# Graph network kernel: general visits of the counts at the head, degrees and bias ahead of a last scatter done by halves, GpSimd left with the gathers

## The chip, the cores and the metric

One Trainium2 chip, one core. The metric is the device time of one execution in microseconds; the number shown is the median of several runs. The profile is that of one execution, and its times are microseconds from the start of its span.

## What is computed

There are 1024 nodes of 128 features and 32768 edges, sorted by their destination. Two layers follow each other, each with a residual. The first is a message-passing layer, the second a graph convolution:

```python
h = jnp.maximum(_layernorm(x), 0.0)
messages = mlp3(concat[h[src], h[dst], edge_attr])
summed = segment_sum(messages, src) + segment_sum(messages, dst)
attention = concat[paired[:, 0] - paired[:, 1], paired[:, 1] - paired[:, 0]]
x = x + mlp3(concat[h, summed, attention])
h = jnp.maximum(_layernorm(x), 0.0)
deg = segment_sum(ones, col)                  # edges and one loop per node
norm = rsqrt(deg)[row] * rsqrt(deg)[col]
x = x + gelu(segment_sum(norm * (h @ W)[row], col) + b)
```

## The kernel before

**Head.** The first layer of the message network is taken apart: `h` times the source and the destination part of `mW1` gives two tables of 1024 x 256, which go to memory. GpSimd gathers their rows for the edges, 128 at a time, by indirect DMAs (L451, L459). Beside this TensorE makes the node's own part of the update (`update_of_node`, L558), ScalarE adds its bias (L895), and VectorE works out from the sorted destinations in which tiles of edges each window lies (L1186 to L1211, turned into a row by `turn_starts`, L511). It then makes the middles and half gaps of the edges' ends (`middles`, L1213).

**Loop over groups.** A group is 512 edges, four tiles of 128; there are 64. The loop is unrolled, and each engine has its own order of a group's steps, written out by hand (`group`, L689 for TensorE, L857 for ScalarE, L1042 for VectorE). In group g TensorE does the second layer of g (L612), the first layer of g + 1 (edge part L592, transposes of the gathered rows L598), the messages of g (L622), and scatters the messages of g - 1 (L640) into two banks that hold the sums for 512 nodes each. For the scatter of a tile an incidence matrix of 128 edges x 1024 nodes is made: ScalarE takes the distance of each node from the middle of the edge's ends (L827), VectorE compares it with the half gap (L1039). For the last tile of a group ScalarE makes the incidence itself in two further passes (L833, L842). For tiles 0 and 2 VectorE's operands are laid out in three rows of 342 (`IN_ROWS`). VectorE also adds the two gathered rows of each edge (`add_pairs`, L1080), makes the low parts of numbers that are multiplied in two parts (L1013, L1019, L1025), and TensorE's first transpose of a group waits for the first half of `add_pairs`.

**Counts.** The graph convolution needs the matrix of edge counts, 1024 x 1024 (`ct_sb`), and the degrees. The destinations are cut into 32 windows of 32 nodes, each window into ten tiles of edges. For each tile VectorE makes two one-hot matrices (`one_hot`, L1088 and L1089), and TensorE multiplies them in among the transposes (`count_tile`, L658). A window takes two groups, five tiles in each; VectorE makes the one-hots a group ahead. When a window is done, ScalarE copies its counts out of PSUM (`window_out`, L887), and VectorE sums them by rows and by columns (`window_sums`, L1108, L1110). Where a window has more than ten tiles, the rest is added by general visits in a loop whose length is read at run time (`more_windows`, L663 and L1113); it always makes at least one visit. It stands after the last window, between the second layer of group 63 and the scatter behind it.

**End.** After it TensorE sums the column counts (`count_ends`, L676), VectorE makes the degrees and the bias times the number of messages (`degrees`, L1174), and TensorE adds that to the sums after the last scatter (`add_bias_of_sums`, L684). ScalarE copies one half of the sums (L904), VectorE the other (L1270), and the update (L726, L732, L740), the second layer norm, the product with the counts (L777) and the output follow. GpSimd, after its last gather, adds the last update bias to `x` (L479) and the identity to the diagonal of the counts (L484, L486).

**What sets the order.** Engines run their instructions in order and wait on semaphores. The queue of SP holds the loads, two loads of edges per group, and the stores; GpSimd's holds the gathers. A gather waits only for its ring buffer of three groups (`GB`).

## Time and profile before

| | us |
|---|---|
| median of 3 runs | 765.26 |
| the runs | 765.11, 765.26, 767.28 |
| the profiled execution, its own time | 768.67 |
| its span | 766.8 |
| busy: TensorE | 741.0 (97%) |
| busy: VectorE | 688.5 (90%) |
| busy: ScalarE | 650.0 (85%) |
| busy: GpSimd | 540.6 (71%) |

Share is of the span. In the rows PE is TensorE, PEld its weight loads, DVE is VectorE, ACT ScalarE, POOL GpSimd. A line number after L is the line of the kernel before. An entry in square brackets at the end of a timeline's row is the idle time of the engine just before that instruction, and what released it. Rows of the chain give net time along the chain, so that an instruction which overlaps the one before it counts only with what it adds. "Granted clock" is the share of TensorE's full clock, 1.00 for 2.4 GHz and 0.50 for 1.2 GHz.

### The profile page before, as it was taken

What the parts mean: (1) busy time and instruction counts of PE and PEld (TensorE: products, weight loads), DVE (VectorE), ACT (ScalarE), POOL (GpSimd) and SP (SyncE); (2) the same over time, 40 slices, a digit from 0 to 9 for tenths busy, and PEclk for the clock granted to TensorE, in tenths of its full rate; (3) what the DMA queues carried; (4) which work ended last, traced back from release to release, by engine and by line L of the source; (5) the groups of instructions that cost most, each with busy time, mean ns of one, the idle gap of its engine ahead of it and who ended that gap; (6) DMA issues with size and microseconds to landing.
All of it is one profiled execution on the core that took longest, in us unless ns stands there. A gap on an engine that the chain in (4) does not pass through costs nothing.

```text
span 766.8 us, 13408 instructions
## 1 busy us (share of the span) xinstructions
PE 741.0 (97%) x4171; PEld 624.5 (81%) x4171; DVE 688.5 (90%) x1444; ACT 650.0 (85%) x839; POOL 540.6 (71%) x533
## 2 busy tenths in 40 slices
PE   7589999999999999999999999999999999999996
PEld 6468888888888888888888888888888888888755
DVE  7869899999999999899998999989999999999765
ACT  3358899999999999999999999999999999998843
POOL 3677777777777777777777777777777777777100
PEclk9789999999999999999999999999999999999999
DMA  8434334444344443344434444344433444442000
GB/s 230 152 115 127 118 112 126 136 125 129 113 124 130 121 133 114 116 134 128 126 109 125 131 131 125 111 123 131 131 122 107 130 135 128 123 118 84 1 0 28
DMA packets 42566, 90.15 MB, mean 118 GB/s; under 512 B 11136, under 2 KB 17920, under 8 KB 42496
## 3 DMA queue, kind: packets, MB, share of 16 engines
q0 software_dynamic: 24576, 67.14, 28.8%
q1 hardware_dynamic: 17920, 22.16, 9.9%
q8 instruction: 33, 0.54, 0.3%
q14 instruction: 37, 0.30, 0.1%
HBM read 86.64 MB, written 2.62 MB: 116 GB/s over the span
## 4 chain that ended last, share of the span: by engine, by line
PE 85%; POOL 7%; issue 2%; DVE 2%; DMA 1%; ACT 1%; DVEq 0%; SPq 0%; POOLq 0%
PE bank L640 29%; PE bank L612 21%; PE bank L622 14%; PE bank L592 7%; PE bank L598 7%; PE bank L658 4%; POOL rows_sb L451 3%; POOL rows_sb L459 3%; PE bank L732 1%; PE bank L777 1%; DMA table_a<-rows_sb 1%; DMA rows_sb<-table_b,ends_i 1%; PE bank L740 1%; PE bank L726 0%; DVE rows_sb L960 0%
## 5 line engine op out<-in xcount | busy, mean ns | idle before, releaser
L459 POOL DMA_INDIRECT rows_sb<-table_b,ends_i x256 | 266.8, 1042 | 78.0 <-issue 78.0
L451 POOL DMA_INDIRECT rows_sb<-table_a,ends_i x256 | 261.4, 1021 | 83.7 <-issue 77.7
L827 ACT ACTIVATE dist<-iota_h,neg_mid 128x1026 f16<-128x1026 f16 (+1 forms) x256 | 294.1, 1150 | 0.0
L1039 DVE TENSOR_SCALAR ring<-dist,half_gap,times 128x1026 fp32r<-128x1026 f16 (+1 forms) x192 | 224.7, 1171 | 0.3 <-ACT dist L827 0.3
L640 PE MATMUL bank<-ring,m_hi 128*128 128x512 f32 x512 | 172.8, 419 | 0.1
L640 PE MATMUL bank<-ring,m_lo 128*128 128x512 f32 x512 | 161.6, 397 | 0.0
L612 PE MATMUL bank<-ring,w_hi 128*128 128x512 f32 x512 | 151.3, 397 | 1.4 <-DVE ring L1019 1.4
L814 ACT ACTIVATE h_sb<-bank,b_sb 128x512 f32<-128x512 f32 x128 | 87.5, 684 | 59.1 <-PE bank L612 59.1
L1089 DVE TENSOR_SCALAR oh_key<-iota_h,key_f,minus_base 128x258 bf16<-128x258 f16 x321 | 128.9, 401 | 0.0
L622 PE MATMUL bank<-w_sb,h_sb 128*128 128x128 f32 x1024 | 125.8, 276 | 0.0
L598 PE MATMUL bank<-ident,rows_sb 128*128 128x128 f32 x512 | 114.3, 277 | 8.0 <-DVE rows_sb L1080 8.0
L622 PEld LDWEIGHTS bank<-w_sb,h_sb 128*128 128x128 f32 x1024 | 120.7, 193 | 0.2
L612 PEld LDWEIGHTS bank<-ring,w_hi 128*128 128x128 f32 x512 | 96.9, 190 | 24.6 <-DVE ring L1019 2.0
L640 PEld LDWEIGHTS bank<-ring,m_lo 128*128 128x128 f32 x512 | 97.5, 190 | 23.3
L1019 DVE SCALAR_TENSOR_TENSOR ring<-bank,ring 128x512 fp32r<-128x512 f32 x128 | 88.3, 690 | 26.6 <-ACT ring L808 25.0
L1080 DVE TENSOR_TENSOR rows_sb<-rows_sb 128x512 f32<-128x512 f32 x128 | 84.2, 685 | 25.0 <-DMA rows_sb<-table_b,ends_i 24.9
L640 PEld LDWEIGHTS bank<-ring,m_hi 128*128 128x128 f32 x512 | 87.7, 191 | 11.7 <-issue 0.2
L1088 DVE TENSOR_SCALAR oh_low<-iota_h,low_f 128x128 bf16<-128x128 f16 x321 | 86.5, 270 | 2.4 <-issue 2.3
L808 ACT ACTIVATE ring<-bank 128x512 fp32r<-128x512 f32 x128 | 76.1, 594 | 14.3 <-PE bank L598 14.3
L598 PEld LDWEIGHTS bank<-ident,rows_sb 128*128 128x128 f32 x512 | 70.6, 143 | 20.2 <-DVE rows_sb L1080 10.2
L612 PE MATMUL bank<-ring,w_lo 128*128 128x512 f32 x256 | 80.8, 397 | 0.0
L842 ACT ACTIVATE ring<-dist,times,neg_times 128x1024 fp32r<-128x1024 f16 x64 | 79.5, 1243 | 0.1
(186 smaller groups left out, 783.6 us busy)
## 6 DMA issues: line engine op xcount, KB each, us to landing
e_raw<-edge_attr_t SPq DMA_DIRECT2D x128, 128.0 KB
rows_sb<-table_a,ends_i POOLq DMA_INDIRECT x256, 2.8
rows_sb<-table_b,ends_i POOLq DMA_INDIRECT x256, 2.9
table_a<-rows_sb SPq DMA_DIRECT2D x4, 256.0 KB, 3.5
table_b<-rows_sb SPq DMA_DIRECT2D x4, 256.0 KB, 3.0
x_sb<-x SPq DMA_DIRECT2D x2, 256.0 KB, 3.3
out<-oh_key SPq DMA_DIRECT2D x4, 128.0 KB, 1.8
u_sb<-uW SPq DMA_DIRECT2D x1, 384.0 KB, 5.0
```

Source lines behind the costliest of these rows:

```text
L451: nc.gpsimd.indirect_dma_start(got[:, b, t, 0, :], None, table_a, bass.IndirectOffsetOnAxis(ap=ends_i[:, 0, tile:tile + 1], axis=0),).then ...
L459: nc.gpsimd.indirect_dma_start(got[:, b, t, 1, :], None, table_b, bass.IndirectOffsetOnAxis(ap=ends_i[:, 1, tile:tile + 1], axis=0),).then ...
L598: mm = nc.tensor.matmul(z1t_bank[k][:, t * P:(t + 1) * P], got[:, g % GB, t, 0, part], ident[:, :], start=False, stop=True, is_transpose=T ...
L612: mm = nc.tensor.matmul(z2_bank[m][:, :], w[:, k, m * P:(m + 1) * P], a[:, b, k, :], start=(n == 0), stop=(n == len(parts) - 1))
L622: mm = nc.tensor.matmul(msg_bank[:, t * D:(t + 1) * D], h2_sb[:, k, t * P:(t + 1) * P], w3_sb[:, k, :], start=(t == 0 and k == 0), stop=(k ...
L640: mm = nc.tensor.matmul(acc_bank[n][:, :], part[:, b, t, :], inc[:, t, n * HB:(n + 1) * HB], start=(is_first(g) and t == 0 and part is m_h ...
L814: nc.scalar.activation(h2_sb[:, m, :], z2_bank[m][:, :], ACT.Relu, bias=b2_sb[:, m:m + 1]).then_inc(h2_ready, 1)
L827: nc.scalar.activation(to, of, ACT.Abs, bias=neg_mid[:, bass.ds(g * GT + t, 1)]).then_inc(dist_ready, 1)
L1019: nc.vector.scalar_tensor_tensor(h1_lo[:, b, k, :], z1t_bank[k][:, :], 0.0, h1_hi[:, b, k, :].bitcast(F32), ALU.max, ALU.subtract).then_in ...
L1039: nc.vector.tensor_scalar(to, of, half_gap[:, tile], times[:, tile], ALU.is_equal, ALU.mult).then_inc(inc_ready, 1)
L1088: nc.vector.tensor_scalar(oh_low[:, slot, j, :], iota_h[:, 0:P], low_f[:, bass.ds(tile, 1)], None, ALU.is_equal)
L1089: return nc.vector.tensor_scalar(oh_key[:, slot, j, :, 0:KN], iota_h[:, 0:KR * KN].rearrange("p (r n) -> p r n", r=KR), key_f[:, bass.ds(t ...
```

## The change

**Order of the counts.** Half-windows take the place of windows in the loop. Half-window h is counted in group h (before: in group h - 1); in groups 16, 33 and 48 two half-windows are counted, so that the last is counted in group 60 (before: 62). VectorE makes a half-window's one-hots a group ahead, interleaved as before; the second one of a doubled group is made in one piece at the end of VectorE's group.

```diff
-LAST_W = 2 * (NW - 1)
...
-def made_in(i):
...
-    return 0 <= i and i + 1 < NW
...
-def summed_in(b, i):
...
-    return b == 0 and 0 <= i < NW
+TWICE = (16, 33, 48)
...
+def counted_in(g):
...
+    first = g + sum(g > x for x in TWICE)
+    found = (first, first + 1) if g in TWICE else (first,)
+    return [h for h in found if 0 <= h < HALVES]
...
+def made_in(g):
...
+    return counted_in(g + 1)
...
+def summed_in(g):
...
+    found = [h // 2 for h in counted_in(g) if h % 2]
+    return found[0] if found else None
...
+LAST_SUM = HALVES - 1 - len(TWICE)
...
+def all_on_vector(g):
...
+    return g >= GROUPS - 2
...
+def in_rows(g, t):
...
+    return t in IN_ROWS and not all_on_vector(g)
```

**GpSimd.** What stood behind the gathers is taken out.

```diff
-    pool.wait_ge(ld_w, 16 * 12)
-    nc.gpsimd.tensor_tensor(xb_sb[:, :, :], x_sb[:, :, :],
-                            ub3_all[:, :].unsqueeze(1).broadcast_to([P, NC, D]), ALU.add).then_inc(xb_ready, 1)
...
-    pool.wait_ge(into_ready, 1)
-    diagonal = ct_all[:, 0:(NC - 1) * (N + P)].rearrange("p (s n) -> p s n", n=N + P)[:, :, 0:P]
-    nc.gpsimd.tensor_tensor(diagonal, diagonal, ident[:, :].unsqueeze(1).broadcast_to([P, NC - 1, P]), ALU.add)
-    diagonal = ct_all[:, (NC - 1) * (N + P):NC * N]
-    nc.gpsimd.tensor_tensor(diagonal, diagonal, ident[:, :], ALU.add).then_inc(self_added, 1)
```

**TensorE.** The row of window starts is turned inside the update of nodes, the general visits come ahead of the loop, the count of ends goes into group 61, and the last scatter is done for the first 512 nodes and then for the others, behind the bias.

```diff
+        if k == KH * NH - 2:
+            turn_starts()
...
-                count_tile(counting[0], counting[1] * (VT // 2) + t - COUNTS_AT[k][0] + k * len(COUNTS_AT[0]))
+                count_tile(counting[0], t + k * len(COUNTS_AT[0]))
...
+        if k == KH - 1:
+            for h in counting[1:]:
+                for j in range(HALF):
+                    count_tile(h, j)
...
     def wait_incidence(g, t):
-        if t < DT:
+        if all_on_vector(g):
+            pe.wait_ge(inc_ready, DT * (GROUPS - 2) + GT * (g - GROUPS + 2) + (t + 1))
+        elif t < DT:
...
-    def counts_of(g):
...
-        w = (g + 1) // 2
-        return (w, (g + 1) % 2) if 0 <= w < NW else None
...
-    def count_tile(w, j):
...
-        if j % (VT // 2) == 0:
-            pe.wait_ge(w_hot, 2 * w + j // (VT // 2) + 1)
+    def count_tile(h, j):
...
+        w, j = h // 2, h % 2 * HALF + j
+        if j % HALF == 0:
+            pe.wait_ge(w_hot, h + 1)
...
     def more_windows():
-        pe.wait_ge(w_out, NW)
...
-            mm = nc.tensor.matmul(acc_bank[c // 4][:, (c % 4) * P:(c % 4 + 1) * P], cb3[:, c, :], ident[:, :],
-                                  start=False, stop=(c % 4 == 3), is_transpose=True, skip_group_check=True)
-            if c % 4 == 3:
-                mm.then_inc(sums_ready, 1)
+            nc.tensor.matmul(acc_bank[c // 4][:, (c % 4) * P:(c % 4 + 1) * P], cb3[:, c, :], ident[:, :],
+                             start=False, stop=False, is_transpose=True, skip_group_check=True)
...
+    def last_scatter(g, b):
...
+        pe.wait_ge(m_lo_ready, g + 1)
+        for n in range(NH):
+            for t in range(GT):
+                if n == 0:
+                    wait_incidence(g, t)
+                for part in (m_hi, m_lo):
+                    mm = nc.tensor.matmul(acc_bank[n][:, :], part[:, b, t, :], inc[:, t, n * HB:(n + 1) * HB],
+                                          start=False, stop=(t == GT - 1 and part is m_lo),
+                                          skip_group_check=True)
+            mm.then_inc(sums_ready, 1)
     def group(g, b, i):
...
+        if g == GROUPS:
+            add_bias_of_sums()
+            last_scatter(g - 1, 1 - b)
+            return
...
-        if g == LAST_W + 1:
-            more_windows()
...
-            first_layer(g + 1, 1 - b, i + b, 0, counts_of(g))
+            first_layer(g + 1, 1 - b, i + b, 0, counted_in(g))
...
-            first_layer(g + 1, 1 - b, i + b, 1, counts_of(g))
+            first_layer(g + 1, 1 - b, i + b, 1, counted_in(g))
...
-        if g == LAST_W + 1:
-            count_ends()
...
+        if g == LAST_SUM + 1:
+            count_ends()
+        if past:
...
-    turn_starts()
+    pe.wait_ge(rows_ready, 1)
+    more_windows()
...
-    pe.wait_ge(rows_ready, 1)
...
-    add_bias_of_sums()
```

**ScalarE.** At the head it clears the counts and writes the diagonal. In the last two groups it no longer makes the incidence of tile 3, and nowhere copies counts.

```diff
     def distance(g, t):
...
-        if t < DT:
+        if is_first(g) and t == 0:
+            act.wait_ge(mids_ready, 1)
...
+        if t < DT or g == GROUPS - 1:
...
-        if t in IN_ROWS:
+        if in_rows(g, t):
...
-        if past:
+        if past and not all_on_vector(g - 1):
...
-        if past:
+        if past and not all_on_vector(g - 1):
...
-        if summed_in(b, i):
-            window_out(i)
...
-    def window_out(w):
...
-        act.wait_ge(w_psum, w + 1)
-        nc.scalar.copy(ct_sb[:, :, bass.ds(w * WD, WD)],
-                       bank[2][:, 0:WK].rearrange("p (d a) -> p a d", a=NC)).then_inc(w_out, 1)
...
+    act.wait_ge(dve_step, 2)
+    for c in range(NC):
+        nc.scalar.activation(ct_sb[:, c, :], iota_h[:, 0:N], ACT.Copy, scale=0.0).then_inc(ct_zero, 1)
+    act.wait_ge(ct_zero, NC)
+    act.wait_ge(consts_pool, 7)
+    diagonal = ct_all[:, 0:(NC - 1) * (N + P)].rearrange("p (s n) -> p s n", n=N + P)[:, :, 0:P]
+    nc.scalar.copy(diagonal, ident[:, :].unsqueeze(1).broadcast_to([P, NC - 1, P])).then_inc(ct_zero, 1)
+    nc.scalar.copy(ct_all[:, (NC - 1) * (N + P):NC * N], ident[:, :]).then_inc(ct_zero, 1)
...
-    act.wait_ge(mids_ready, 1)
...
-        if t in IN_ROWS:
+        if in_rows(g, t):
```

**VectorE.** General visits and their sums at the head, the middles later and in two parts, a window's counts added to what is there, tile 3 of the last two groups, and the bias of the update added to `x` at the end.

```diff
     def group(g, b, i):
...
-        makes = made_in(i)
-        if makes:
-            tile0 = window_tile(i + 1)
-            one_hots(i + 1, tile0, b, (0, 1))
+        makes = made_in(g)
+        if makes and exists(g):
+            h = makes[0]
+            tile0 = window_tile(h // 2)
+            one_hots(h, tile0, (0, 1))
...
-        if makes:
-            one_hots(i + 1, tile0, b, (2,))
+        if makes and exists(g):
+            one_hots(h, tile0, (2,))
...
+        if past and all_on_vector(g - 1):
+            incidence(g - 1, 3)
...
+        if g == FIRST + 1:
+            middles_done()
...
-        if makes:
-            one_hots(i + 1, tile0, b, (3,))
+        if makes and exists(g):
+            one_hots(h, tile0, (3,))
...
-        if makes:
-            one_hots(i + 1, tile0, b, (4,))
+        if makes and exists(g):
+            one_hots(h, tile0, (4,))
...
-        if summed_in(b, i):
-            window_sums(i)
+        for more in makes[1 if exists(g) else 0:]:
+            one_hots(more, window_tile(more // 2), range(HALF))
+        if summed_in(g) is not None:
+            window_out(summed_in(g))
...
-    def one_hots(w, tile0, half, tiles):
...
+    def one_hots(h, tile0, tiles):
...
+        w, half = h // 2, h % 2
...
-            j = half * (VT // 2) + t
+            j = half * HALF + t
...
-            if t == VT // 2 - 1:
+            if t == HALF - 1:
...
-    def window_sums(w):
...
+    def window_out(w):
...
+        dve.wait_ge(w_psum, w + 1)
+        counts = ct_sb[:, :, bass.ds(w * WD, WD)]
+        found = bank[2][:, 0:WK].rearrange("p (d a) -> p a d", a=NC)
+        nc.vector.tensor_tensor(counts, counts, found, ALU.add).then_inc(w_out, 1)
...
-        counts = ct_sb[:, :, bass.ds(w * WD, WD)]
...
     def more_windows():
-        dve.wait_ge(w_sums, NW)
+        dve.wait_ge(ct_zero, NC + 2)
...
-        STEPS = 15
+        STEPS = 11
...
-            then(nc.vector.tensor_reduce(add_into[:, :], counts.rearrange("p (d a) -> p d a", a=NC),
-                                         AX_X, ALU.add))
-            then(nc.vector.tensor_reduce(add_from[:, :], counts.rearrange("p (d a) -> p a d", a=NC),
-                                         AX_X, ALU.add))
...
-            to = into_part[:, bass.ds(w * WD, WD)]
-            then(nc.vector.tensor_tensor(to, to, add_into[:, :], ALU.add))
-            to = from_part[:, bass.ds(w, 1), :].rearrange("p w a -> p (w a)")
-            then(nc.vector.tensor_tensor(to, to, add_from[:, :], ALU.add))
-            dve.wait_ge(more_step, v * STEPS + done[0])
...
+    def sum_counts():
...
+        dve.wait_ge(w_sums, NW)
...
     def degrees():
...
-        step(nc.vector.tensor_copy(deg_in[:, :], bank[2][:, HB // 2 + HC * 4:HB // 2 + HC * 4 + NC]))
+        step(nc.vector.tensor_copy(root[:, 1, :], bank[2][:, HB // 2 + HC * 4:HB // 2 + HC * 4 + NC]))
+        dve.wait_ge(into_ready, 1)
...
-        step(nc.vector.tensor_scalar(root[:, 1, :], deg_in[:, :], 1.0, None, ALU.add))
-        dve.wait_ge(into_ready, 1)
-        step(nc.vector.tensor_tensor(cnt[:, :], deg_in[:, :], deg_out[:, :], ALU.add))
+        step(nc.vector.scalar_tensor_tensor(cnt[:, :], root[:, 1, :], -2.0, deg_out[:, :], ALU.add, ALU.add))
...
+    def middles_done():
...
-        dve.wait_ge(mids_ready, 1)
...
-    middles()
...
+    more_windows()
...
-    tile0 = window_tile(0)
-    for half in range(2):
-        one_hots(0, tile0, half, range(VT // 2))
...
-    run_groups(dve, group, FIRST + 1, {1: count_passes, LAST_W: more_windows, LAST_W + 1: degrees})
+    middles()
+    run_groups(dve, group, FIRST + 1, {1: count_passes, LAST_SUM: sum_counts, LAST_SUM + 1: degrees})
...
-    dve.wait_ge(self_added, 1)
+    dve.wait_ge(w_out, NW)
...
+    dve.wait_ge(ld_w, 16 * 12)
+    nc.vector.tensor_tensor(xb_sb[:, :, :], x_sb[:, :, :],
+                            ub3_all[:, :].unsqueeze(1).broadcast_to([P, NC, D]), ALU.add).then_inc(xb_ready, 1)
```

Not shown: names of semaphores and buffers that come or go, and the whole numbers that GpSimd writes, which lie in `dist` and no longer in the first rows of the counts.

## Rows read from the trace of the kernel before

**Rows 1.** The page's fourth part: the chain that ended last, by engine

```profile
PE 85%; POOL 7%; issue 2%; DVE 2%; DMA 1%; ACT 1%; DVEq 0%; SPq 0%; POOLq 0%
```

**Rows 2.** Windows: core 0, 100 to 700 us; busy (count) of PE, PEld, DVE, ACT, POOL; clock; DMA; GB/s

```profile
100.00:700.00 600.00, 600.00 (x3431) 510.90 (x3431) 559.50 (x1126) 551.25 (x704) 462.94 (x451) 1.00 0.41 124
```

**Rows 3.** Timeline of TensorE at 90 us: start, length, line, operation, tile, idle before, releaser

```profile
90.71 0.44 PE L598 MATMUL bank<-ident,rows_sb 128*128 128x128 f32 x2 [1.08 <-DVE rows_sb L1080]
```

**Rows 4.** The page's fifth part: the gathers of table_b

```profile
L459 POOL DMA_INDIRECT rows_sb<-table_b,ends_i x256 | 266.8, 1042 | 78.0 <-issue 78.0
```

**Rows 5.** Chain in order of time, 690 to 767 us: start, us, what

```profile
695.07 2.79 PE bank L612 x12
...
699.44 0.94 PE bank L640 x4
...
701.15 1.79 PE bank L622 x16
...
721.24 1.78 PE bank L640 x4
723.02 2.77 PE bank L622 x16
725.79 1.68 PE bank L676 x16
```

**Rows 6.** Timeline of TensorE, last group and update

```profile
716.26 0.62 PE L612 MATMUL bank<-ring,w_hi 128*128 128x512 f32 x2
...
720.88 0.28 PE L669 MATMUL bank<-oh_key,oh_low 128*128 128x258 bf16 x1 [1.67 <-DVE oh_key L1089]
...
735.19 3.70 PE L726 MATMUL bank<-rows_sb,u_sb 128*128 128x512 f32 x8 [0.24 <-ACT rows_sb L904]
```

**Rows 7.** Timeline of ScalarE, last group

```profile
719.47 0.68 ACT L814 ACTIVATE h_sb<-bank,b_sb 128x512 f32<-128x512 f32 x1
...
726.31 3.23 ACT L827 ACTIVATE dist<-iota_h,neg_mid 128x1024 f16<-128x1024 f16 x3
```

**Rows 8.** Timeline of VectorE, between two groups with a window's sums

```profile
204.31 0.24 DVE L1088 TENSOR_SCALAR oh_low<-iota_h,low_f 128x128 bf16<-128x128 f16 x1
...
204.79 0.24 DVE L1088 TENSOR_SCALAR oh_low<-iota_h,low_f 128x128 bf16<-128x128 f16 x1
...
205.99 1.28 DVE L1080 TENSOR_TENSOR rows_sb<-rows_sb 128x512 f32<-128x512 f32 x2
```

**Rows 9.** Timeline of TensorE at the transposes of the same rows

```profile
207.83 0.27 PE L598 MATMUL bank<-ident,rows_sb 128*128 128x128 f32 x1
...
208.27 0.38 PE L598 MATMUL bank<-ident,rows_sb 128*128 128x128 f32 x2
```

**Rows 10.** Timeline of VectorE, the general visit

```profile
717.36 0.23 DVE L1128 TENSOR_SCALAR over_f<-rows_f,visit_f 1x32 f32<-1x32 f32 x1 [0.84 <-DVE from_part L1110]
...
721.88 0.41 DVE L1152 TENSOR_TENSOR ct_sb<-ct_sb,bank 128x256 f32 x1
```

**Rows 11.** Windows, TensorE alone: stretch, sum, busy (count), granted clock, DMA share, GB/s

```profile
89.60:90.80 1.20, 0.12 (x2) 1.00 0.39 109
719.20:721.20 2.00, 0.29 (x2) 1.00 0.00 0
722.00:724.50 2.50, 2.50 (x11) 0.50 0.00 0
```

**Rows 12.** Timeline of VectorE and of GpSimd behind the last gather

```profile
704.90 3.22 DVE L1039 TENSOR_SCALAR ring<-dist,half_gap,times 128x1024 fp32r<-128x1024 f16 x1
...
705.16 2.39 POOL L479 TENSOR_TENSOR x_sb<-x_sb,ub_all 128x1024 f32<-128x1024 f32 x1
```

**Rows 13.** Timeline of ScalarE and VectorE at the head, and of VectorE before the residual

```profile
21.72 0.69 ACT L895 ACTIVATE uh_sb<-bank,ub_sb 128x512 f32<-128x512 f32 x1 [7.06 <-PE bank L576]
...
45.06 0.69 DVE L1080 TENSOR_TENSOR rows_sb<-rows_sb 128x512 f32<-128x512 f32 x1 [4.33 <-DMA rows_sb<-table_b,ends_i]
...
745.93 0.69 DVE L1282 TENSOR_TENSOR rows_sb<-bank,x_sb 128x512 f32<-128x512 f32 x1 [3.91 <-PE bank L740]
```

More of the change, by code:

```diff
@@ L47, in gnn_preln_kernel @@
     KR, KN, KP = 3, 86, 88
+    HALF = VT // 2
+    HALVES = 2 * NW
     MORE = NW * TILES
@@ L163, in gnn_preln_kernel @@
         from_part = sb("from_part", [P, NW, NC])
-        add_into = sb("add_into", [P, WD])
-        add_from = sb("add_from", [P, NC])
         deg_out = sb("deg_out", [P, NC])
-        deg_in = sb("deg_in", [P, NC])
         cnt = sb("cnt", [P, NC])
@@ L195, in gnn_preln_kernel @@
         w1_hi, w1_lo = inc[:, 1, 0:2 * H], inc[:, 1, 2 * H:4 * H]
-        iota_f = ct_sb[:, 0, :]
+        iota_f = dist[:, :, :].rearrange("p t n -> p (t n)").bitcast(F32)[:, 0:N]
         xb_sb = x_sb
@@ L252, in gnn_preln_kernel @@
         w_out = sem("w_out")
+        ct_zero = sem("ct_zero")
         w_sums = sem("w_sums")
@@ L296, in gnn_preln_kernel @@
         zero_ready = sem("zero_ready")
-        self_added = sem("self_added")
         ct_pass = sem("ct_pass")
```

## The prediction

> **What bounds the kernel now.** I read the chain of work that ended last first: TensorE holds 85% of it, and GpSimd, the next, 7% [rows 1]. Then the busy time of the long middle stretch: from 100 to 700 us TensorE is busy in all 600.00 us, VectorE in 559.50, ScalarE in 551.25 [rows 2]. So in the loop over groups any TensorE work that is added or removed counts in full, and so does any wait it is given; work added to VectorE counts only where VectorE then comes late for TensorE. A group takes some 10.6 us (from 695.07 to 716.26, the starts of two second layers [rows 5, 6], two groups pass); VectorE has 0.7 us a group left (40.5 us over some 56 groups).
>
> Ahead of that the gathers set the pace. TensorE's last wait before 700 us is 1.08 us at 90.71, for rows that VectorE had just added [rows 3]. GpSimd gathers without a pause but 0.30 us between two (78.0 us of idle time over 256 gathers of table_b), 1.04 us each [rows 4], so eight of them take 10.7 us, as long as TensorE's group. From 90.71 on TensorE is never late for them, but not by much.
>
> At the end TensorE waits again, 1.67 us for the one-hots of the general visit [rows 6].
>
> **The end: a gain of 4.0 us.** Before, the second layer of group 63 starts at 716.26 [rows 6] and takes 2.79 (twelve matmuls [rows 5]), to 719.05. The first scatter after it starts at 721.24: 2.19 us lost to the visit. It then takes 1.78 where the same four matmuls take 0.94, and the messages take 2.77 where they take 1.79 [rows 5]: 0.84 + 0.98 = 1.82 us more, because the granted clock is 0.50 in this stretch (1.2 of 2.4 GHz), after TensorE had been busy in 0.29 of 2.00 us [rows 11]. With the visit at the head, wait and slow stretch go. The messages will then wait for ScalarE's second ReLU: it ended at 719.47 + 0.68 = 720.15 [rows 7], the scatter would end at 719.05 + 0.94 = 719.99; I take 0.2. The count of ends (16 matmuls, 1.68 us [rows 5]) is not saved, only moved to group 61, where TensorE is as full. The scatter by halves moves the bias ahead of the last scatter; its matmuls are the same, and what goes is the wait of 0.24 us for ScalarE's copy of the first half of the sums [rows 6], since that copy now runs beside the second half. Sum: 2.19 - 0.20 + 0.84 + 0.98 + 0.24 = 4.05.
>
> What is late next there? The last scatter needs tile 3 of group 63. ScalarE makes a distance in 1.08 us (3.23 for three [rows 7]), VectorE an incidence tile in 0.72 (205.27, the end of two one-hots, to 205.99 [rows 8]); counting from the messages' end at about 722.0, ScalarE's copy and three distances end at 725.9, the tile at 726.7, and TensorE comes to it at 727.1 (after 2.8 us of scatter, 0.9 of bias, three tiles of 0.47). It holds by 0.4; bounds -0.4 to +0.4. The two reductions that wait for the counts, and the degrees, wait in VectorE's queue behind group 61's work for the count of ends, with the next rows to add behind them; TensorE is itself 1.68 us later there, so I take 0.
>
> **Work taken off GpSimd: nothing.** Adding the bias to x there held up VectorE: its incidence tile took 3.22 us beside GpSimd's 2.39 us operation [rows 12]. The Trainium skill, page "SBUF — State Buffer", section "Who interferes with whom", says that the two share one pair of ports and that the second to come is blocked outright; the 3.22 us agree. Read by that rule alone the move would give about 2.4 us. TensorE shows no wait there, so the sum by the rows has 0: VectorE has room at that point. On VectorE the addition costs 1.28 (as two of L1080 [rows 8]), inside the 3.91 us for which it waits before the residual [rows 13]. The diagonal adds were off the path too. No DMA moves, and nothing is put into the queues of SP or GpSimd.
>
> **Counts added by VectorE, not copied by ScalarE.** Each of 32 windows gets an addition of 0.41 us (the same operation is L1152 [rows 10]) and a wait for its own end, 0.45 together, behind which stand the two reductions, the next one-hots, an incidence tile and the rows to add. At the end of such a group VectorE is ahead: the first pair of rows is added at 205.99 + 0.64 = 206.63, and TensorE takes it at 207.83 [rows 8, 9]. The slack is 1.20 us, and 0.45 of it goes. Cost 0; bounds 0 and, where gathers have eaten the slack, 0.1 in each of a dozen groups, 1.2.
>
> **The three doubled groups: a loss of 5.5 us, and the clock.** To be two groups earlier with the last window, five tiles' one-hots more are made at the end of VectorE's groups 15, 32 and 47, each behind the group's low messages and ahead of the next rows to add. Each of the three also has a window's sums in it (half-windows 15, 33 and 49 are odd ones). A tile costs 0.48 us (204.31 to 204.79 [rows 8]), five 2.40; with the 0.45 above VectorE is 2.85 us late against a slack of 1.20, so TensorE waits 1.65 at its first transpose. The second pair is added 0.64 later; TensorE reaches it after 0.44 [rows 9] and waits 0.20 more. That is 1.85 a group, 5.55 for three. TensorE cannot make it up. Bounds: 0, were VectorE to find room that the rows don't show, and with the clock's fall 3 x (1.85 + 1.82) = 11.0.
>
> Does the clock fall? After 1.67 us of waiting it did, for 1.82 us [rows 5, 11]; in the 1.08 us wait at 90.71 it stayed at 1.00 [rows 11]. A wait of 1.65 and one of 0.20 close behind are nearest to the first, but the fall need not come each time; I take half: 1.5 x 1.82 = 2.7.
>
> **The head: 0.** ScalarE clears the counts (8 x 1.08 us and a copy of the diagonal, about 10) in a wait of 7.06 us [rows 13], so the update of nodes ends some 2.5 us later. The visit took VectorE 717.36 to 722.29 [rows 10]; four of its steps go, some 4.4 us are left, with the load of its count 5.2. ScalarE is free from 21.72 - 7.06 = 14.66, and done at about 24.5, so by this estimate the visit lasts to 30; edges and the first three middles end at 32, when the first rows are about there. Then the second half of the middles, 2.4, stands before the first low part, but the five tiles of one-hots now come behind it; the second layer of group 0 starts 0.5 later. Behind it VectorE waited 4.33 us for gathers at 45.06 [rows 13], and TensorE 1.08 at 90.71. These cover it. Without that cover it would be the 0.5, and at most the visit's 5 us. The gathers' own start doesn't depend on it. Bounds: -1.1 (the wait at 90.71, should the gathers come earlier) to +1.5.
>
> **Sum.** -4.05 + 5.55 + 2.73 = +4.2 us. The profiled execution took 768.67 us, its span 766.8; the median of the runs is 765.26, 3.4 lower. Against its own time that makes 772.9; I put the same step on the median: 769.5.
>
> **Rivals.**
> (a) The clock holds in all three waits: -4.05 + 5.55 = +1.5, 766.8. For it speaks the wait of 1.08 without a fall; against it the wait of 1.67 with one.
> (b) The doubled groups cost nothing, and it gets faster: 765.26 - 4.05 = 761.2. The place is the end of VectorE's groups 15, 32 and 47, the price 1.85 each, and the point from which it decides is a lateness of 1.20 us. For it: VectorE has 0.7 us a group to spare on the mean. Against it: all three are groups with sums, and low messages wait for TensorE, so earlier slack can't be saved up.
> (c) The head or the gathers lose more: the visit's chain through three engines ends after the first rows, or the gathers, already as long as a group, get slower beside one-hots that stand closer. 2.5 us more than the forecast, 772. Against it: the cover above, and the stalls of the doubled groups give the gathers time.
>
> **Chances.** The forecast (waits, and the clock falls in one to three of them) 0.55, (a) 0.20, (b) 0.17, (c) 0.08. The forecast's own range is 768 to 772.5. To leave out no more than 2 in 10 the whole range goes from (b), 761.0, to 773.0, the fall in all three (772.2) with the bounds of the head. About 0.3% (2.3 us) is what a measurement of this kernel can tell from no change. Slower by more: 0.50 of the forecast's, 0.05 of (a), 0.07 of (c): 0.62. Faster by more: 0.15 of (b) and 0.03 of (a): 0.18. The rest, 0.20, within.
>
> **What would show it.** Right: TensorE waits of 1.6 to 2 us before a transpose of rows (L598 before) near 218, 402 and 566 us, released by VectorE's addition of rows; granted clock 0.50 for some microseconds behind some of them; no wait between the last two second layers and the last scatter, and 13.3 us instead of 18.9 from the start of group 63's second layer to the first update matmul; count of ends about 1.7 us in group 61. Wrong: no such waits (then it is (b)); waits but the clock at 1.00 (a); a last wait for gathers later than 90.7 or a first second layer later than about 39.5 (c); a wait inside the last scatter (tile 3 late).

## The result, and the profile after

The changed kernel takes 769.2 us (median of 20 runs, 766.35 to 771.71) against 766.4 us for the kernel before, run beside it (20 runs, 765.11 to 770.27): ratio 1.0033, 95% interval 1.0022 to 1.0044, so slower by 2.8 us (1.7 to 3.4). The profiled execution took 769.43 us, its span 767.5.

The chain of waits is still TensorE's, by engine (85% before [rows 1]):

```profile
PE 86%; DVE 4%; POOL 3%; issue 3%; ACT 2%; DMA 1%; DVEq 0%; POOLq 0%
```

The window that had TensorE busy throughout [rows 2] now has 4.8 us of idle time in it (busy time of PE, PEld, DVE, ACT, POOL, granted clock, DMA, GB/s):

```profile
100.00:700.00 600.00, 595.23 (x3410) 506.00 (x3408) 565.93 (x1162) 537.60 (x668) 464.30 (x446) 1.00 0.41 123
```

It lies in three places. TensorE's timeline at the transposes of gathered rows (start, length, line, operation, idle before, releaser):

```profile
216.65 0.40 PE L600 MATMUL bank<-e_parts,w1e_lo 128*128 128x512 f32 x1
218.60 0.33 PE L606 MATMUL bank<-ident,rows_sb 128*128 128x128 f32 x1 [1.55 <-DVE rows_sb L1109]
...
402.49 0.33 PE L606 MATMUL bank<-ident,rows_sb 128*128 128x128 f32 x1 [1.60 <-DVE rows_sb L1109]
...
565.06 0.33 PE L606 MATMUL bank<-ident,rows_sb 128*128 128x128 f32 x1 [1.61 <-DVE rows_sb L1109]
```

VectorE's timeline ahead of the first of them says why. The second half-window's five one-hot tiles begin at 212.49, the counts are added at 214.90, and the rows at last at 217.87:

```profile
212.49 0.24 DVE L1117 TENSOR_SCALAR oh_low<-iota_h,low_f 128x128 bf16<-128x128 f16 x1
...
214.90 0.40 DVE L1139 TENSOR_TENSOR ct_sb<-ct_sb,bank 128x256 f32<-128x256 f32 x1
215.33 0.61 DVE L1141 TENSOR_REDUCE into_part<-ct_sb 128x32 f32<-128x256 f32 x1
...
217.87 1.28 DVE L1109 TENSOR_TENSOR rows_sb<-rows_sb 128x512 f32<-128x512 f32 x2
```

The tiles take 2.41 us and the addition 0.43: these are the prediction's 2.40 and 0.45, late against a slack that the trace before had at 1.20 [rows 8, 9]. But the clock does not fall behind the waits (TensorE alone: stretch, its length, busy time, granted clock, DMA, GB/s; the fourth row is the end, from the edge part of group 63 to the first matmul of the update):

```profile
218.60:222.60 4.00, 4.00 (x30) 1.00 0.22 66
402.50:406.50 4.00, 4.00 (x30) 1.00 0.24 70
565.00:569.00 4.00, 3.94 (x30) 1.00 0.22 66
715.50:736.10 20.60, 20.54 (x114) 1.00 0.01 1
```

In the head, TensorE's last wait for gathered rows comes at 55.60; near 90, where the first profile before has one [rows 3], there is none (nor is there in the second profile before, below):

```profile
55.60 0.44 PE L606 MATMUL bank<-ident,rows_sb 128*128 128x128 f32 x2 [2.73 <-DVE rows_sb L1109]
```

At the end the visit's wait and the 0.50 clock [rows 6, 11] are gone. TensorE's timeline: the count of ends, the second layer of group 63, the first of the last scatter, the update:

```profile
710.00 1.84 PE L685 MATMUL bank<-ones_col,into_part 128*128 128x1 f32 x16
711.70 0.72 PE L654 MATMUL bank<-ring,m_hi 128*128 128x512 f32 x2
...
722.84 0.63 PE L624 MATMUL bank<-ring,w_hi 128*128 128x512 f32 x2
...
732.30 0.48 PE L704 MATMUL bank<-ring,m_hi 128*128 128x512 f32 x1
...
736.09 3.60 PE L747 MATMUL bank<-rows_sb,u_sb 128*128 128x512 f32 x8
```

From the second layer to the update it is 736.09 - 722.84 = 13.25 us, against 735.19 - 716.26 = 18.93 before [rows 6]; 1.68 us of the difference are the count of ends [rows 5], which only moved to group 61. VectorE's wait before the residual was 3.91 [rows 13]; now 1.22 us of added bias stand there, and 2.77 of waiting are left:

```profile
742.74 1.22 DVE L1302 TENSOR_TENSOR x_sb<-x_sb,ub_all 128x1024 f32<-128x1024 f32 x1
746.73 0.69 DVE L1310 TENSOR_TENSOR rows_sb<-bank,x_sb 128x512 f32<-128x512 f32 x1 [2.77 <-PE bank L761]
```

**Reading a stall from the group pitch.** The loop is so regular that the start of each group's edge part (L600) measures every loss to 0.02 us: 10.67 us from one group to the next, which is called the pitch here. In the changed kernel it is 13.14 after group 17 (215.96 to 229.10), 13.20 after groups 34 and 49, 11.92 after group 62 (the count of ends), 10.67 elsewhere behind group 3. All experiments below are read by this ruler.

### The profile page after: what moved, and what is told of

Same layout as the page of the kernel before. It is cut to its first block, busy times and chain, and to the rows that moved or that the text cites. A ratio compares the mean times of both kernels' runs of the same rounds, so it can differ in the third digit from the quotient of the medians.

```text
span 767.5 us, 13409 instructions
## 1 busy us (share of the span) xinstructions
PE 739.5 (96%) x4171; PEld 622.3 (81%) x4171; DVE 696.2 (91%) x1474; ACT 645.1 (84%) x813; POOL 538.5 (70%) x530
## 4 chain that ended last, share of the span: by engine, by line
PE 86%; DVE 4%; POOL 3%; issue 3%; ACT 2%; DMA 1%; DVEq 0%; POOLq 0%
PE bank L654 29%; PE bank L624 21%; PE bank L634 14%; PE bank L606 7%; PE bank L600 7%; PE bank L668 4%; POOL rows_sb L467 2%; POOL rows_sb L475 1%; PE bank L753 1%; PE bank L798 1%; DMA table_a<-rows_sb 1%; DVE oh_low L1117 1%; DVE oh_key L1118 1%; ACT dist L850 1%; PE bank L761 1%
## 5 line engine op out<-in xcount | busy, mean ns | idle before, releaser
L467 POOL DMA_INDIRECT rows_sb<-table_a,ends_i x256 | 267.0, 1043 | 83.5 <-issue 77.7
L850 ACT ACTIVATE dist<-iota_h,neg_mid 128x1024 f16<-128x1024 f16 (+1 forms) x256 | 293.7, 1149 | 0.0
L1061 DVE TENSOR_SCALAR ring<-dist,half_gap,times 128x1026 fp32r<-128x1026 f16 (+1 forms) x194 | 221.6, 1142 | 5.0 <-ACT dist L850 4.9
L654 PE MATMUL bank<-ring,m_hi 128*128 128x512 f32 x504 | 169.0, 416 | 0.0
L654 PE MATMUL bank<-ring,m_lo 128*128 128x512 f32 x504 | 158.8, 396 | 0.0
L606 PE MATMUL bank<-ident,rows_sb 128*128 128x128 f32 x512 | 112.5, 277 | 8.6 <-DVE rows_sb L1109 8.6
L654 PEld LDWEIGHTS bank<-ring,m_lo 128*128 128x128 f32 x504 | 95.4, 189 | 22.2
L654 PEld LDWEIGHTS bank<-ring,m_hi 128*128 128x128 f32 x504 | 85.9, 190 | 11.5
L865 ACT ACTIVATE ring<-dist,times,neg_times 128x1024 fp32r<-128x1024 f16 x62 | 76.9, 1240 | 0.0
```

The costliest lines, as they stand in the source:

```text
L467: nc.gpsimd.indirect_dma_start(got[:, b, t, 0, :], None, table_a, bass.IndirectOffsetOnAxis(ap=ends_i[:, 0, tile:tile + 1], axis=0),).then ...
L606: mm = nc.tensor.matmul(z1t_bank[k][:, t * P:(t + 1) * P], got[:, g % GB, t, 0, part], ident[:, :], start=False, stop=True, is_transpose=T ...
L654: mm = nc.tensor.matmul(acc_bank[n][:, :], part[:, b, t, :], inc[:, t, n * HB:(n + 1) * HB], start=(is_first(g) and t == 0 and part is m_h ...
L850: nc.scalar.activation(to, of, ACT.Abs, bias=neg_mid[:, bass.ds(g * GT + t, 1)]).then_inc(dist_ready, 1)
L1061: nc.vector.tensor_scalar(to, of, half_gap[:, tile], times[:, tile], ALU.is_equal, ALU.mult).then_inc(inc_ready, 1)
```

## Experiments

The theory: three stalls of nearly 2 us from VectorE's lateness, no clock loss, a smaller end. The rivals: the stalls carry a clock loss that one profile happens not to show; the head differs; the gathers bind.

**The changed kernel again** (no edit).

> The changed kernel once more, beside the others of this call. Theory (each doubled group costs TensorE one wait of 1.6 us and 0.2 to 0.3 more behind it, 5.8 us for the three; the clock does not fall there): 1.0033 of the kernel before, three TensorE waits of 1.55 to 1.6 us, granted clock 1.00 behind all of them. Rival (the clock falls behind the wait in some executions, and the profile shown was one without): 0.50 for some microseconds behind at least one of the three in this profile too.

769.29 us, ratio 1.0032 [1.0016, 1.0048] to the kernel before. The same three waits, 1.58 to 1.62, groups of 13.19 to 13.22, and a granted clock of 1.00 behind each.

**Five tiles spread over the three turns ahead.**

```diff
-                for more in makes[1 if exists(g) else 0:]:
-                    one_hots(more, window_tile(more // 2), range(HALF))
...
+                for ahead, tiles in ((3, (0,)), (2, (1, 2, 3)), (1, (4,))):
+                    if g + ahead in TWICE:
+                        h = counted_in(g + ahead)[1]
+                        one_hots(h, window_tile(h // 2), tiles)
```

> The five tiles of the second half-window of each doubled group are no longer made in one piece at the end of VectorE's group d-1, but one at the end of group d-3, three at the end of d-2 and one at the end of d-1. Same work on every engine. Theory (lateness of VectorE against a slack of 1.2 us, or 0.75 with the window's addition, sets the wait): the three waits go, 5.8 us, to about 763.4 us, 0.996 of the kernel before, and faster than it. Rival (the five added matmuls of a doubled group, or the gathers, make the wait): the waits stay, 1.003.

766.17 us, ratio 0.9998 [0.9980, 1.0016]: about half of the gain expected. The waits are short but not gone:

```profile
218.02 0.33 PE L606 MATMUL bank<-ident,rows_sb 128*128 128x128 f32 x1 [0.25 <-DVE rows_sb L1114]
...
400.96 0.33 PE L606 MATMUL bank<-ident,rows_sb 128*128 128x128 f32 x1 [0.21 <-DVE rows_sb L1114]
```

The doubled groups are 11.81 to 11.86 long instead of 13.14 to 13.20, but each of the two groups ahead is now some 0.2 longer: three turns are late. In the changed kernel the second addition of rows ends 0.56 us ahead of TensorE in a turn that also sums a window, 1.78 in the others; with one tile ahead of it the first comes 0.66 later, with three the second 1.89. A tile still costs 0.48 there, as in the prediction. In the first turn, which sums a window, the incidence tile of 1024 starts 0.48 later, and it then takes 1.00 us instead of 0.80, beside a gather that had begun before it (0.98 and 0.99 at the other two places):

```profile
194.20 1.00 DVE L1061 TENSOR_SCALAR ring<-dist,half_gap,times 128x1024 fp32r<-128x1024 f16 x1
```

In the second turn VectorE is 0.46 late against TensorE's edge part before the tiles begin, left over from the first turn, and three tiles add 1.43. So the turns ahead have less room than their slack in the changed kernel says: lateness is handed from one turn to the next. (The expectation of the early tiles below puts a tile at about 0.6 us; the rows have 0.48.)

**Two doubled groups, 16 and 33** (`TWICE = (16, 33)`).

> Two doubled groups (16 and 33) in place of three; the last window then ends a group later, the count of ends comes into group 62, and the degrees are made behind VectorE's group 62. Theory: 1.9 us less than the changed kernel, about 767.3, 1.0008 of the kernel before, with no new wait at the end because the bias is only needed after group 63. Rival (the degrees, one group later, are late for the bias): a wait before the bias, 1.002 or more.

767.47 us, ratio 1.0009 [0.9993, 1.0026], as expected: one stall less is worth 1.8 us, between the 769.29 and this.

**The same stall made longer**: four more one-hot tiles in each doubled group, into a buffer that nobody reads.

> In the three doubled groups VectorE makes four tiles of one-hots more, into a buffer that nobody reads, 1.9 us each. Theory: each of the three waits grows by 1.9, to about 3.5 us, 5.8 us in all, to 775, 1.011 of the kernel before, if the clock holds; if it falls behind waits of 3.5 us, as it did behind the wait of 1.67 us at the end of the kernel before, 1.8 more each, up to 780, 1.018. Rival (VectorE has room behind the doubled groups): less than 1.005.

778.06 us, ratio 1.0157 [1.0131, 1.0183], in between. The waits are alike, the clock behind them is not:

```profile
218.43 0.47 PE L608 MATMUL bank<-ident,rows_sb 128*128 128x128 f32 x1 [3.55 <-DVE rows_sb L1120]
...
405.70 0.33 PE L608 MATMUL bank<-ident,rows_sb 128*128 128x128 f32 x1 [3.59 <-DVE rows_sb L1120]
...
571.75 0.33 PE L608 MATMUL bank<-ident,rows_sb 128*128 128x128 f32 x1 [3.58 <-DVE rows_sb L1120]
```

```profile
218.40:221.20 2.80, 2.77 (x10) 0.51 0.33 101
405.70:409.20 3.50, 3.50 (x14) 0.57 0.32 94
571.70:575.20 3.50, 3.45 (x25) 1.00 0.14 49
```

The three groups last 16.55, 16.70 and 15.17: a fall costs 1.4 to 1.5 us here, and with a wait of 3.6 us it came in two of three, in this one profile.

**Tiles into a buffer of their own, only in turns with room.** The second half-window gets five tiles of its own (`early_low`, `early_key`, with a semaphore `early_hot`), so that they can be made further ahead:

```diff
+                for ahead, tiles in ((6, (0, 1)), (4, (2, 3)), (2, (4,))):
+                    if g + ahead in TWICE:
+                        early_hots(counted_in(g + ahead)[1], tiles)
...
+                low = early_low[:, j % HALF, :] if early else oh_low[:, w % HOT, j, :]
+                key = early_key[:, j % HALF, :, 0:KN] if early else oh_key[:, w % HOT, j, :, 0:KN]
```

> The second half-window of each doubled group gets its own small buffer (5 tiles), and VectorE makes two of its tiles at the end of its turn six groups before, two four groups before and one two groups before: all turns ahead of an addition that has the longer slack (1.78 us in the changed kernel's trace against 0.56 in the turns that also sum a window; a tile takes about 0.6). My theory now: the run before this one (tiles spread over the three turns just ahead) won only part because one tile is already more than the 0.56 us of a summing turn. Expected: no wait at the three groups, each of which is then longer than an ordinary group by the 0.54 us of its five count matmuls alone (11.21 us from edge part to edge part, after 13.14); ratio to the kernel before about 0.996 (763.4 us), about 5.8 us under the changed kernel. Rival: the head takes the rest, and the ratio stays at about 0.999 to 1.000, although the waits are gone.

763.64 us, ratio 0.9972 [0.9954, 0.9989]: faster than both kernels, 2.2 us under the kernel before where 2.9 were expected. VectorE's lateness is gone: groups 34 and 49 are 11.22 and 11.21 long, the 0.54 of their count tiles and no more. What is left is neither theory nor rival: gathers. VectorE waits for one, and TensorE for VectorE (the second addition, near 625 us):

```profile
625.52 0.69 DVE L1124 TENSOR_TENSOR rows_sb<-rows_sb 128x512 f32<-128x512 f32 x1 [1.84 <-DMA rows_sb<-table_b,ends_i]
```

```profile
626.27 0.44 PE L611 MATMUL bank<-ident,rows_sb 128*128 128x128 f32 x2 [0.48 <-DVE rows_sb L1124]
```

Groups 17 and 52 to 56 lose 1.85 us together so. In the changed kernel the stalls had hidden this: there the last gather of a group ends on average 5.5 us ahead of the group's edge part, here 3.0 (2.8 in the kernel before; groups from 6 on).

**The bias behind the whole last scatter, no halves.**

```diff
+                    for t in range(GT):
+                        scatter(g - 1, 1 - b, t)
                     add_bias_of_sums()
-                    last_scatter(g - 1, 1 - b)
```

> The bias comes behind the whole last scatter again, and the scatter goes tile by tile over both halves; everything else is as in the changed kernel. Theory: the halves by themselves are worth little: from group 63's second layer to the first update matmul 13.5 to 13.7 us against 13.25, the difference a wait of about 0.3 us of that matmul for ScalarE's copy of the first half. Rival: the halves carry a larger part of the end's gain, and the stretch is 14.3 us or more.

A single run: 770.58 us. The update starts 736.84 - 723.22 = 13.62 us behind the second layer, and the 0.24 us of the kernel before [rows 6] are back:

```profile
736.84 0.70 PE L750 MATMUL bank<-rows_sb,u_sb 128*128 128x512 f32 x1 [0.24 <-ACT rows_sb L929]
```

The halves are worth 0.37 us in these two profiles.

**ScalarE makes the fourth tile in the last groups too** (`return g >= GROUPS` in `all_on_vector`).

> ScalarE makes the fourth incidence tile again in the last two groups too; everything else is as in the changed kernel. Theory: the last scatter then waits for ScalarE's tile, which comes behind its third difference of that group: about 0.9 to 1.1 us between the bias and the end of the last scatter, so 14.2 to 14.4 us from group 63's second layer to the first update matmul, against 13.25. Rival: ScalarE gets it done in time, 13.25 us.

A single run: 772.06 us, and a miss upward: from the second layer to the update 738.86 - 723.07 = 15.79 us, 2.54 more. The expectation forgot one of ScalarE's passes; it needs two behind the last distance (1.15 and 1.24 us), and TensorE waits for two tiles (the first for one of VectorE's):

```profile
734.32 0.50 PE L704 MATMUL bank<-ring,m_hi 128*128 128x512 f32 x1 [0.51 <-DVE ring L1061]
...
736.44 0.50 PE L704 MATMUL bank<-ring,m_hi 128*128 128x512 f32 x1 [1.38 <-ACT ring L865]
```

So without the tile's move to VectorE 2.5 of the end's 4 us would be lost. The edit does one thing more: `all_on_vector` also decides the layout of VectorE's tiles, so tiles 0 and 2 of the last two groups are in three rows again and take 1.34 us instead of 0.81. That is not what sets the 2.54: ScalarE works without a pause from 724.67 until its tile is done at 736.38, and that tile comes last.

**The kernel before, profiled again.**

> The kernel before, unchanged, for a second profile of its head. Group 6's edge part starts at 100.05 us in the first profile of it; in five profiles of the changed kernel's head (itself and the four runs so far) it starts at 98.6, 99.7, 98.9, 97.3 and 96.4. If the change moved the head, this one starts near 100 again; if the head only varies from execution to execution, it can start anywhere from 97 to 100.6 (the kernel before has counted one half-window, 0.54 us, more by then).

A single run: 765.41 us. Group 6's edge part starts at 96.98, against 100.05 in the first profile. So the head varies by 3 us from execution to execution without any change. And at the end the visit's wait is again 1.67 us, but the clock holds:

```profile
717.87 0.28 PE L669 MATMUL bank<-oh_key,oh_low 128*128 128x258 bf16 x1 [1.67 <-DVE oh_key L1089]
```

```profile
716.20:718.20 2.00, 0.29 (x2) 1.00 0.00 0
718.20:720.20 2.00, 1.97 (x13) 1.00 0.00 0
```

**A one-hot tile between the incidence tile and the additions** (on top of the early tiles).

```diff
-                    one_hots(h, tile0, (0, 1))
+                    one_hots(h, tile0, (0,))
                 if past:
                     incidence(g - 1, 1)
+                if makes and exists(g):
+                    one_hots(h, tile0, (1,))
                 if nxt:
                     add_pairs(g + 1)
```

> The kernel of the early tiles elsewhere, with one line moved in VectorE's turn: the second one-hot tile stands between the incidence tile of 1024 and the two additions of rows, not ahead of both. Theory: what eats the rest of that kernel's gain is the gathers, whose pitch there is 10.72 us a group against TensorE's 10.67. In all traces so far a gather that starts while VectorE runs this incidence tile ends 0.82 us after the end of the additions behind it, up to 2.76 us long (17 gathers over 2.2 us in that kernel); parted by a one-hot tile, the 0.8 us and the 1.28 us hold up a gather each for itself, so none should be over about 2.1 us, the pitch falls under 10.6, and TensorE's late waits for gathers (1.8 us in all in that profile) go: ratio to the kernel before 0.994 to 0.996. Rival: the length of gathers has another cause, gathers over 2.2 us stay, and the ratio stays at 0.997.

762.61 us, ratio 0.9955 [0.9937, 0.9973], the lowest median of all. By times alone it can't be told from the early tiles (0.9972 [0.9954, 0.9989]); what shows the step is the trace. TensorE's window is full again:

```profile
100.00:700.00 600.00, 600.00 (x3440) 511.27 (x3439) 573.81 (x1170) 541.96 (x674) 463.20 (x450) 1.00 0.41 123
```

No gather is over 2.07 us, where 17 were over 2.2; every doubled group is 11.20 to 11.22 long, every other 10.67 (but for the count of ends). One expectation failed: the gathers' pitch did not fall under 10.6, it is 10.71. The mean gather is as long as before (1.029 us, 1.033 before); 87 of them instead of 27 take 1.1 to 2.2 us. What changed is that none comes late by itself: between 100 and 700 us VectorE's longest wait for a gather is 0.83 us, where it was 1.84, and TensorE waits for none.

**Another between the two additions** (`one_hots(h, tile0, (2,))` between the halves of `add_pairs`).

> As the last, and the third one-hot tile stands between the two additions. By the same theory no gather is over about 1.6 us, and the pitch of the gathers falls further, to some 10.4; the second addition comes 0.5 us later, which leaves it about 0.05 us of slack in the turns that sum a window (0.55 before), so TensorE may wait 0.1 or so there, 28 times at most: ratio 0.993 to 0.998. It is better than the last only if the gathers still bind there, or in the head, where a long wait for gathers near 53 us goes with a lower granted clock behind it. Rival as above: gathers over 2.2 us stay.

763.53 us, ratio 0.9970 [0.9957, 0.9983]: not to be told from the last. One gather is over 1.6 us (2.53, at 687 us, in a turn that has no one-hots to stand between), and a group's last gather ends 4.5 us ahead of its edge part instead of 2.9; but TensorE waited for no gather in the loop any more, so this buys nothing.

Head and rest of the profiled executions (group 6 by the start of its edge part; the last column is the profiled execution's own device time less that start):

| kernel | median, us | group 6 starts | from there to the end |
|---|---|---|---|
| before (two profiles) | 766.4 | 100.05, 96.98 | 668.6, 668.4 |
| changed (two profiles) | 769.2 | 98.60, 99.72 | 670.8, 671.0 |
| spread over three turns | 766.17 | 98.90 | 667.9 |
| two doubled | 767.47 | 97.27 | 669.8 |
| longer stall | 778.06 | 96.44 | 680.4 |
| early tiles | 763.64 | 98.74 | 667.4 |
| one-hot between | 762.61 | 97.66 | 664.8 |
| additions parted | 763.53 | 100.61 | 665.6 |

## Why the prediction was right, and where it was not

769.5 was forecast and 769.2 came, slower, with the three stalls where and as long as forecast. The clock's fall, which the forecast added to them, did not come in any profile: by its mechanism the outcome is rival (a), which had a chance of 0.20. The sum of +4.2 us was 1.4 too much, and that the number is so near is luck: it was put on a median of three runs (765.26) that 20 runs have at 766.4. Step by step:

**Doubled groups: right.** Forecast 1.85 each. Measured: 2.47, 2.53 and 2.53 over an ordinary group, of which 0.54 are the five count tiles (the doubled group without any wait shows just that), so 1.93 to 1.99 of stall, 5.9 in sum for 5.55. The wait that the trace shows, 1.55, is not all of it. The first transpose starts 1.95 us behind the last matmul of the edge part (216.65 to 218.60), where 0.23 is usual (205.98 to 206.21): 1.72 for the forecast's 1.65. The third, which waits for the second addition, starts 0.61 behind the first (at 219.21), where 0.44 is usual: 0.17 for the forecast's 0.20, without a bracket of its own. Undone, the stalls give their time back: against the kernel before, run beside each, the medians go from +3.0 us to -2.2 with what the gathers take, and to -3.4 without. Rival (b), that they cost nothing, is out.

**The clock: the step that failed.** "Does the clock fall?" was answered with half of the three, "1.5 x 1.82 = 2.7". It measured 0: the clock fell behind none of the 14 waits of 1.55 to 1.62 us in five profiles of kernels with this stall. In this rival (a) was right. The argument rested on one row, a wait of 1.67 us with a fall behind it; the second profile of the same kernel has the same wait without a fall. One execution could not give the price, nor the chance. What decides whether it falls stays open.

**The end: right in its parts, and smaller on the mean.** Forecast -4.05. From the edge part of group 62 to the update: 11.92 + 20.57 in the changed kernel, 10.68 + 26.82 before, 5.01 less; two half-windows that are no longer counted there (1.08) belong to the doubled groups, so -3.93. Against the second profile of the kernel before, whose clock held, it is 10.68 + 25.89, and so -3.0. The forecast's 0.98 + 0.84 for the slow clock is a loss that one of two profiles has. Between the two the scatter and the messages differ by 1.61 us (721.24 to 725.63, against 718.23 to 721.01), and 0.68 of this comes back as a longer last scatter (6.57 us, against 7.25), where TensorE comes sooner and waits for two of VectorE's tiles (they end at 726.70 and 727.95, and TensorE goes on at 726.75 and 728.00). Of the smaller terms the 0.24 for halves measured 0.37; the tile 3 that was to hold by 0.4 ended at 733.4 and was needed at 733.8; the count of ends takes 1.70 us in group 62's pitch (710.00 to 711.70), and no wait arose there.

**The head: 0, right, though not for a reason that one profile could show.** The changed profile's head is 1.45 us earlier than the first one before, and it would be easy to book that as a gain. The profiles of the table vary by over 3 us, with or without the change. Each kernel's median differs from the kernel before by what its last column differs, within about 0.6 us but for one (the early tiles: -2.2 and -1.1; that execution took 2.5 us beyond its span, most others 1.7 to 1.9), and on the mean by 0.1. So the head is neutral to about half a microsecond. The visit's last addition ends at 30.16, where the forecast had 30, and the first second layer starts at 38.39, where it started at 38.54 before: it never came late for the first rows. Which part of the cover hid the visit was not tried.

**Work off GpSimd, counts added by VectorE: 0, right.** TensorE has no wait near the place of GpSimd's addition, before or after; the move was not tried by itself. The 3.22 us show that VectorE's tile was held up for the whole of GpSimd's operation, but not the order that the prediction reads into them: the tile starts 0.26 us ahead of it (704.90 and 705.16 [rows 12]), 0.25 ahead in the second profile. The slack before the second addition went from 1.00 to 0.56 in turns that sum a window, 0.44 for the forecast's 0.45, and no wait of TensorE arose there. It does count in the doubled groups, where it is part of the lateness, as forecast.

The sum as measured: 5.9 - 3.0 (or -3.9) + 0 = +2.9 (or +2.0), for +2.8 (1.7 to 3.4) between the medians, which both sums fit. Rival (c), 772, is out.

## What to carry to other kernels

Work that is moved earlier to empty the end must go where the engine that makes it has room in that very turn: here the turns alternate between 0.56 and 1.78 us of slack, and a mean of 0.7 a group says nothing of where five tiles fit. Lateness that is left over goes on into the next turn. A buffer of its own, 5 tiles large, let them be made in the right turns, and that turned 2.8 us lost into 2.2 gained; one line moved on VectorE for the gathers' sake took the last 1.85 us of waits out of the loop's trace (3.4 by the medians, not clear of the 2.2). And where a loop has a fixed pitch, its start times show every loss to 0.02 us, while two profiles of one kernel can differ by 3 us in the head: read a loss from the pitch, and a head from several profiles.

## What the runs showed of the hardware

**The clock's fall isn't set by the length of the wait alone.** The same 1.67 us wait of the kernel before had a fall behind it in one profile and none in the other; 3.55 and 3.59 had one, 3.58 had none. In the head, near 55 us, TensorE's waits for gathered rows of 1.51, 1.61 and 1.82 us held the clock; those of 2.73 to 2.97 had a fall about them in all seven profiles that have one (and so had two of 1.48 and 0.95 close together, in the first profile before). The longer wait and the fall go together, and with them goes the head: group 6 starts at 96.4 to 97.7 where the clock held, at 98.6 to 100.6 where it fell.

**Two of VectorE's operations hold up GpSimd's gathers, one behind the other.** Most gathers take 0.95 us. One that is caught by the incidence tile of 1024 or by an addition of rows ends 0.82 us after the last operation of the unbroken series. In the twelve traces, between 70 and 700 us, all 199 gathers that start at least 0.1 us behind the start of such an operation and 0.2 us ahead of its end take over 1.0 us, up to 2.76; of 2928 that meet neither these nor an addition of edge parts (64x512, which holds them too) none takes over 1.01. GpSimd's and VectorE's timelines of the changed kernel, at the first stall:

```profile
217.22 2.75 POOL L467 DMA_INDIRECT rows_sb<-table_a,ends_i  x1 [0.30 <-issue]
```

```profile
217.15 0.80 DVE L1061 TENSOR_SCALAR ring<-dist,half_gap,times 128x1024 fp32r<-128x1024 f16 x1
```

The additions behind this tile end at 217.87 + 1.28 = 219.15, the gather at 219.97. With a one-hot tile between (the run with that name), an addition alone does it too: this gather starts 0.13 us behind one and ends 0.83 us after its end (129.21 + 1.27):

```profile
129.34 1.97 POOL L472 DMA_INDIRECT rows_sb<-table_a,ends_i  x1 [0.30 <-issue]
```

```profile
129.21 1.27 DVE L1126 TENSOR_TENSOR rows_sb<-rows_sb 128x512 f32<-128x512 f32 x2
```

The Trainium skill, page "SBUF — State Buffer", section "Who interferes with whom", has an addition with both inputs in SBUF contend with GpSimd's reads, and infers that the making of a gather's descriptors is not held up by it. The 1.97 us disagree with what is inferred, for the gather as a whole, and the measurement decides: here such an addition holds a gather as the incidence tile does. Which part of the gather is held the trace doesn't show. One-hot tiles, and the incidence tiles laid out in three rows, were seen to hold none.
